# A two-layer graph kernel: adjacency passes of 512 neighbouring columns instead of two far panels of 256, ScalarE copies the first ten Z tiles, weight preparation cut into pieces, the first attention panels' relu issued two chunks ahead

## The reference

```
deg = max(rowsum(adj != 0), 1)
x   = layernorm(x + relu(((adj + I) @ x / deg + x) @ W + b))       # layer 0 (degree factor on both sides)
h   = x @ W_sa;  sl = h @ a_left;  sr = h @ a_right
e   = where(adj != 0, exp(-leaky_relu(sl[:, None] + sr[None, :], 0.01)), 0)
x_a = (e / (rowsum(e) + 1e-5)) @ h
x_b = adj @ (x @ W_gcnb) + b_gcnb
ga  = sigmoid([adj @ x, x] @ Wa + ba);  gb = sigmoid([adj @ x, x] @ Wb + bb)
out = layernorm(x + sigmoid(ga * x_a + gb * x_b))
```

## Time and profile before

| quantity | before |
|---|---|
| median of 3 timed executions | 945.04 us (943.79 to 945.75) |
| profiled execution, its own time | 944.09 us |
| profiled execution, span from first to last instruction | 942.3 us |
| PE busy | 901.3 us (96%) |
| DVE busy | 640.2 us (68%) |
| ACT busy | 459.7 us (49%) |
| POOL busy | 87.4 us (9%) |
| DMA, share while the adjacency is read (slices 5 to 13) | 0.8 to 0.9 |

### The profile page before, as it was taken

One profiled execution on the slowest core, in us unless ns is written; L12 is line 12 of the kernel. 1 busy time (PEld: TensorE's weight loads), 2 busy tenths in 40 slices (PEclk: granted clock), 3 DMA queues, 4 the chain that ended last, 5 costly groups with the idle time before them and its releaser, 6 DMA issues.

```text
span 942.3 us, 20464 instructions
## 1 busy us (share of the span) xinstructions
PE 901.3 (96%) x7829; PEld 783.3 (83%) x7829; DVE 640.2 (68%) x1432; ACT 459.7 (49%) x642; POOL 87.4 (9%) x139
## 2 busy tenths in 40 slices
PE   7995799999999999979999999999999999999996
PEld 6874688888888888858888888888888888888885
DVE  6576555544554446777998797797797797797762
ACT  2653455455455324655656365365355455455450
POOL 1020212222212210000000000000000000000000
PEclk8998999999999999979999999999999999999999
DMA  9978899999999400102201110111111211101000
GB/s 303 273 239 266 285 308 329 311 306 338 300 312 332 165 18 18 52 1 74 73 19 68 61 49 35 61 40 44 61 30 54 61 27 56 61 22 59 15 24 12
DMA packets 95784, 121.65 MB, mean 129 GB/s; under 512 B 6480, under 2 KB 91504, under 8 KB 91632
## 3 DMA queue, kind: packets, MB, share of 16 engines
q1 hardware_dynamic: 91120, 116.69, 37.8%
q10 hardware_dynamic: 4608, 4.20, 1.3%
HBM read 95.69 MB, written 25.18 MB: 128 GB/s over the span
## 4 chain that ended last, share of the span: by engine, by line
PE 82%; DVE 9%; ACT 3%; issue 3%; DMA 2%; POOL 0%; SPq 0%; DVEq 0%; ACTq 0%; POOLq 0%
PE ps L1148 32%; PE ps L1031 22%; PE ps L1110 20%; PE ps L1066 4%; DVE ec L866 3%; PE ps L1014 3%; DVE em L875 1%; ACT ec L516 1%; ACT em L519 1%; DMA strip<-in_adj_dram 1%; DMA xs<-in_x_dram 1%; DVE y L640 1%; PE ps L1051 1%; PE ps L1003 1%; DVE codes L600 0%
## 5 line engine op out<-in xcount | busy, mean ns | idle before, releaser
L1148 PE MATMUL ps<-fb,em 128*128 128x257 f16 x3072 | 346.5, 275 | 8.1 <-DVE em L875 8.1
L1148 PEld LDWEIGHTS ps<-fb,em 128*128 128x128 f16 x3072 | 301.4, 98 | 50.9 <-issue 8.6
L1031 PE MATMUL ps<-y,codes 128*128 128x257 f16 x2048 | 245.9, 276 | 11.7 <-DVE lnst L766 7.8
L1031 PEld LDWEIGHTS ps<-y,codes 128*128 128x128 fp8e4 x2048 | 201.8, 99 | 44.9 <-DVE lnst L766 8.1
L1110 PE MATMUL ps<-fa,pan 128*128 128x258 f16 x2048 | 232.4, 273 | 0.9 <-DVE slrow L834 0.9
L1110 PEld LDWEIGHTS ps<-fa,pan 128*128 128x128 fp8e4 x2048 | 199.2, 97 | 30.7 <-DVE slrow L834 1.2
L866 DVE SCALAR_TENSOR_TENSOR ec<-slb,sr,pan 128x256 f32<-128x256 f32 x512 | 207.9, 478 | 7.6 <-issue 7.3
L516 ACT ACTIVATE ec<-ec,sc 128x2048 f32<-128x2048 f32 x64 | 127.9, 1999 | 131.1 <-DVE ec L866 131.1
L875 DVE SCALAR_TENSOR_TENSOR em<-ec,em 128x2048 f16<-128x2048 f32 x64 | 146.4, 2287 | 16.6 <-ACT em L519 16.5
L519 ACT ACTIVATE em<-ec 128x2048 f16<-128x2048 f32 x64 | 122.3, 1911 | 8.2
L738 DVE TENSOR_SCALAR lnst<-ps 128x1 f32<-128x1 f32 x32 | 5.0, 157 | 107.9 <-PE ps L1031 107.9
(11 more groups left out here) (99 smaller groups left out, 503.0 us busy)
## 6 DMA issues: line engine op xcount, KB each, us to landing
strip<-in_adj_dram SPq DMA_DIRECT2D x128, 512.0 KB, 6.2
a_scratch<-codes SPq DMA_DIRECT2D x16, 1024.0 KB, 8.4
pan<-a_scratch SPq DMA_DIRECT2D x16, 1024.0 KB, 5.0
x_scratch<-x ACTq DMA_DIRECT2D x32, 128.0 KB, 4.7
x1r<-x_scratch SPq DMA_DIRECT2D x32, 128.0 KB, 2.1
out_dram<-ot SPq DMA_DIRECT2D x32, 128.0 KB, 1.7
xs<-in_x_dram SPq DMA_DIRECT2D x3, 1024.0 KB, 11.0
slb<-sl_scratch SPq DMA_DIRECT2D x16, 128.0 KB, 4.7
```

The source lines that it names most:

```text
L1031: mm = pe.matmul(ACC(n), codes[:, qq % SLOTS, h, jb, e * P:(e + 1) * P].bitcast(F8), y[:, jb, part, :], start=(jb == 0 and part == 0), sto ...
L1148: mm = pe.matmul(PH(b)[:, 0:HC], em[slot][:, e_part, jb, (b % 2) * P:(b % 2 + 1) * P], fb[:, jb, h_part, :], start=(jb == 0 and e_part + h ...
```

## The change

Passes now hold 512 neighbouring columns (panels 2qq and 2qq + 1), so a strip is two row blocks of 512 columns where it was four of 256, tiles follow in natural order, and `TILES` is gone. SP sends both halves of a pass's codes to DRAM together, after the pass's last strip. A row block of pass 0 now needs one strip for all four tiles. ScalarE copies Z of tiles 0 to 9 (`ZACT`), VectorE of the rest, after all six `x_max` and `z_scale`. `y_hi` and `y_lo` catch up two a step and then follow two tiles behind. `OUTER` is 16 in place of 24: pass 0 sums row blocks 16 to 31 after the ramp. The weight steps are called at t = 18 to 22, 26, 28, 29 and 30. The first transpose and projection stand inside and behind pass 0. In the first two panels of the second layer the order on VectorE is relu(i), then low(i - 2), across both panels.

The sizes, and the strips and codes on SP:

```
-SJ = 4
+SJ = 2
+ZACT = 10
-OUTER = 24
+OUTER = 16
...
-                sp.dma_start(strip[:, s % RING], adj_view[:, g * SJ:(g + 1) * SJ, c0:c0 + PW]
+                sp.dma_start(strip[:, s % RING], adj_view[:, g * SJ:(g + 1) * SJ, qq * 2 * PW:(qq + 1) * 2 * PW]
...
-                if s >= RING and ends(s - RING):
-                    codes_when_cast(s - RING)
+                if s >= RING and (s - RING) % GS == GS - 1:
+                    codes_when_cast((s - RING) // GS)
```

On ScalarE and VectorE, which `y` parts fall in a step, and ScalarE's steps and what follows them:

```
+        def split_at(t):
+            upto = lambda i: 0 if i < ZACT else min(i - 1, 2 * (i - ZACT) + 2)
+            return range(upto(t - 1), T if t == T else upto(t))
...
             for t in range(T):
                 xt_copy(t)
-                if t >= YLAG:
-                    y_hi(t - YLAG)
-                if 8 <= t < 24 and t % 2 == 0:
+                if 1 <= t <= ZACT:
+                    z_copy(t - 1)
+                for i in split_at(t):
+                    y_hi(i)
+                if 9 <= t < 25 and t % 2 == 1:
                     cast(1)
...
-            cast(6)
-            for n in range(3):
-                normalize(n)
+            cast(4)
+            normalize(0)
             cast(2)
+            x1t_copy(0)
+            normalize(1)
+            cast(2)
+            proj_copies(0)
```

On VectorE, the ramp and what follows it:

```
-            for c in range(4):
+            for c in range(len(XCUT) - 1):
                 x_max(c)
-            for t in range(T):
+            st.sync()
+            dve.tensor_reduce(sc[:, XMX], sc[:, XM], AX, ALU.max).then_inc(S["xmax_part"], 1)
+            z_scale()
+            for t in range(ZACT, T):
                 z_copy(t)
-                if t >= YLAG:
-                    y_lo(t - YLAG)
+                for i in split_at(t):
+                    y_lo(i)
+                if 18 <= t < 22:
+                    weight_column((t - 18) // 2, t % 2)
                 if t == 22:
-                    weight_columns()
+                    weight_squares()
                 if t == 26:
                     weight_norm()
-                if t == 30:
+                if t == 28:
                     weight_scale()
+                if t in (29, 30):
+                    weight_parts(t - 29)
...
-            cast(6)
-            for n in range(3):
-                head(n)
+            cast(2)
+            head(0)
+            cast(2)
+            head(1)
```

On TensorE, the end of the ramp and of pass 0:

```
-                if t - 1 >= ZLAG:
+                if 0 <= t - 1 - ZLAG < OUTER:
                     pass0_rows(t - 1 - ZLAG)
-            for jb in range(T - ZLAG, OUTER):
-                pass0_rows(jb)
             pe.wait_ge(S["ylo_ready"], T)
             for n in range(PT):
                 sum_rows(n, OUTER, T)
+                if n == 2:
+                    t_step(0)
+            p_step(0)
```

More of the change, by code:

```diff
@@ L55 @@
 PER_PAIR = 4 * 5
-TILES = [2 * q + h * (T // 2) + e for q in range(NQ) for h in range(2) for e in range(2)]
 BASE = 16512
@@ L302, in _ @@
                 sp.dma_start(slb[:, m, :], sl0d[m * PW:(m + 1) * PW].partition_broadcast(P)).then_inc(slb_in[m], 16)
-            for s in range(NSTRIP - RING, NSTRIP):
-                if ends(s):
-                    codes_when_cast(s)
+            codes_when_cast(NQ - 1)
             sp.wait_ge(S["slrow_ready"], 1)
@@ L429, in xt_copy, with z_copy @@
                 act.copy(xt[:, t % 2, :], XTP(t)).then_inc(S["xt_ready"], 1)
+            def z_copy(t):
+                act.wait_ge(S["z_done"], t + 1)
+                act.copy(zf[:, t, 0:D], ZP(t)).then_inc(S["zf_act"], 1)
             def y_hi(t):
-                act.wait_ge(S["zf_ready"], t + 1)
+                z_is_copied(act, t)
                 if t == 0:
@@ L568, in _ @@
             for e in range(2):
-                gates(e, 0, 0, e)
+                gates(e, 0, e)
                 gated(e, e)
@@ L684, in weight_scale, with weight_parts @@
                 dve.tensor_scalar(sc[:, INVA], sc[:, IAL], 1.0 / EDGE_VAL, None, ALU.mult).then_inc(S["alpha_ready"], 1)
+            def weight_parts(part):
+                st.sync()
+                if part == 0:
+                    st.then(dve.tensor_scalar(wps[:, :, 0, :], wp[:], sc[:, WS], None, ALU.mult))
+                else:
+                    dve.scalar_tensor_tensor(out=wps[:, :, 1, :], in0=wp[:], scalar=sc[:, WS], in1=wps[:, :, 0, :],
+                                             op0=ALU.mult, op1=ALU.subtract).then_inc(S["wps_ready"], 1)
@@ L771, in head, with parts_lo @@
                 stats(n)
-            cast(6)
-            for n in range(3):
-                head(n)
+            def parts_lo(n):
+                g_lo(n)
+                h_lo(n)
             cast(2)
-            for n in range(PT, T + 3):
-                if n == PT:
-                    x1t_lo(0)
-                    head(3)
-                    g_lo(0)
-                    h_lo(0)
-                    x1t_lo(1)
-                    cast(2)
-                    continue
-                if n == PT + 1:
-                    g_lo(1)
-                    h_lo(1)
-                    x1t_lo(2)
-                    head(4)
-                    g_lo(2)
-                    h_lo(2)
-                    x1t_lo(3)
-                    cast(2)
-                    continue
+            head(0)
+            cast(2)
+            head(1)
+            cast(2)
+            x1t_lo(0)
+            head(2)
+            cast(2)
+            head(3)
+            parts_lo(0)
+            x1t_lo(1)
+            cast(2)
+            parts_lo(1)
+            x1t_lo(2)
+            parts_lo(2)
+            x1t_lo(3)
+            head(4)
+            cast(2)
+            for n in range(PT + 2, T + 3):
                 more = n // PT + 1 < NQ and n < T
@@ L1016, in z_step, with rows_cast @@
                 mm.then_inc(S["z_done"], 1)
-            def rows_cast(qq, h, jb):
-                s = next(i for i in range(NSTRIP) if strip_at(i) == (qq, h, jb // SJ))
-                mine = 0 if on_act(s) else 1
-                pe.wait_ge(S[("cast_act", "cast_dve")[mine]], casts_until(s)[mine])
+            def rows_cast(qq, jb):
+                strip_nr = qq * GS + jb // SJ
+                mine = 0 if on_act(strip_nr) else 1
+                pe.wait_ge(S[("cast_act", "cast_dve")[mine]], casts_until(strip_nr)[mine])
             def sum_rows(n, j0, j1):
@@ L1104, in a_rows @@
             def a_rows(b, slot, j0, j1):
-                for j in range(j0, j1):
-                    jb = TILES[j]
+                for jb in range(j0, j1):
                     for part in range(2):
                         mm = pe.matmul(PA(b)[:, 0:GC], pan[:, slot, jb, (b % 2) * P:(b % 2 + 1) * P].bitcast(F8),
-                                       fa[:, jb, part, :], start=(j == 0 and part == 0),
-                                       stop=(j == T - 1 and part == 1))
+                                       fa[:, jb, part, :], start=(jb == 0 and part == 0),
+                                       stop=(jb == T - 1 and part == 1))
                 return mm
```

208 lines of the change are left out of this document (88 added, 120 removed).

## The result

The changed kernel takes 929.92 us in the median (929.85 to 929.98, 4 runs) beside 945.27 (943.79 to 945.75, 4 runs) for the kernel before: a ratio of 0.984, 95% interval 0.9823 to 0.9857. The forecast was 929.5, with 921 to 938 as its range. The profiled execution has a span of 928.1 us where it was 942.3, and a mean granted clock of 0.988 where it was 0.983.

A forecast was written before the change was run, and what follows sets the result against it. TensorE was busy 901.3 of 942.3 us, so nearly all to win lay in its 41 idle us. 944.09 less 15.9 (up to tile 6) plus 0.4 (second layer) gave 928.6; with 0.95 for the median, 929.5, range 921 to 938.

The forecast's parts named there:

- Ramp to z12: Start of the ramp: with ScalarE copying Z, z12 starts at 24.7 instead of 28.26, 3.6 us won.
- z12 to z31: Later ramp: 16 paces of 1.98 us bring z28 at 56.3; z29 and z30 follow at 57.4 and 58.5.
- The power: GpSimd's power near the ramp's end: ends at 62.2, VectorE waits 4.3 us, all `y_lo` done at 68.6.
- The reading that in the ramp the gap starts at the end of this sum: GpSimd in the ramp: power ends 9.8 us after L359's end at 52.5; counting from the maximum also gave 62.2.
- Rest of pass 0: After the ramp up to tile 6: it starts at 106.1, with 0.2 us waiting at the second projection; 15.9 us won.
- the last lands near 87, in front of the third head's end: Handover after pass 0: the last of strips 22 to 31 arrives near 87, before the third head ends.
- about 4 us from a freed buffer to landing: Handover strips 22 to 31: each takes about 4 us from freed buffer to landing, one coming in 1.5 us.
- The rival of the sticky handover: Handover after pass 0: late strips make TensorE wait twice, some 3.5 us each; win falls about 7, 936.5 us; chance 0.16.
- Passes: Steady passes: tile pitch stays 8.73 us and VectorE's cast 689 ns, nothing on the path either way.
- the slower rival: Steady passes: codes leaving as one 2 MB piece delay strips and stall all six passes, 950.5 us at 3.5 each; chance 0.05.
- Second layer: Its first panels: waits of 2.2, 2.0 and 4.3 us, 2.4 lost to clock; net -0.4, between -1.5 and +2.0.
- Sum: Whole kernel: 944.09 - 15.9 + 0.4 = 928.6 us for the profiled execution, 929.5 for the median of timed runs.

The follow-up runs named there:

- the warmed power: Changed kernel plus one unused GpSimd power after the last maximum over partitions, before the second layer's loop: 925.35 us, ratio 0.978.
- the first experiment: Changed kernel with the weight scale and both weight parts moved behind the last `y_lo`: 928.15 us, ratio 0.9814.
- the fourth version: Changed kernel with late weight steps, casts through the ramp (ScalarE's last behind the last `y_hi`) and an unused GpSimd power before layer two's loop: 917.61 us, ratio 0.9716.
- the last pair: the fourth version, 917.61 us, and the same kernel with `OUTER = 20` in place of 16, 917.05 us.

## Why the prediction was right, point by point

**Ramp to z12.** Forecast 24.7, measured 23.87: the first cast started at 18.24 and the last piece of the maximum at 16.89, both sooner than the rate of 348 GB/s had given. The experiment that undoes the copies confirms the place and the direction.

**z12 to z31.** The pace stayed at 1.98 and z28 stood at 55.63 against 56.3.

**The power.** Right in kind and too large in size. It ended at 60.05, not at 62.2, and VectorE waited 2.56 us, not 4.3, since the gap was 7.78 us and not 9.24 and the sum over partitions ended at 51.67 and not 52.5. The reading that in the ramp the gap starts at the end of this sum is shown; its length was taken from one execution, and it varies from 7.36 to 9.05. The last y was done at 65.84 and not 68.6: 2.15 of the 2.8 us are the power's, 0.45 the first weight part's, which took 0.75 us where 1.2 was taken.

**Rest of pass 0.** Wrong in the handover, and saved by the term before it. The second projection waited 2.09 us where I had 0.2, and 1.7 us more went to half clock. The step that failed is "the last lands near 87, in front of the third head's end". The last strip was there at 85.6, even a little sooner, but the third head had ended at 82.51 and VectorE stood still for 2.22 us, with the fourth head and `x1t_lo` behind the cast. The "about 4 us from a freed buffer to landing" is near the least in the trace of before (3.8, with 6.2 in the median); from 60 to 100 us the changed kernel's strips took 7.0 in the median. With 2.8 us won at y, 0.4 less lost to the clock behind it and 3.6 more lost here, 106.3 becomes 106.7; the trace has tile 6 at about 106.8. The rival of the sticky handover had the mechanism at about half of its price.

**Passes.** 8.73 us a tile, as forecast; 702 ns a cast against the 689 kept. TensorE has no stall between 107 and 350 us, so codes in one piece of 2 MB cost nothing: the slower rival is out.

**Second layer.** The net of the stretch was -0.6 where -0.4 stood: 2.12, 2.06 and 4.46 us of waiting, 2.7 at half clock, against 2.2, 2.0, 4.3 and 2.4. Neither sign is clear of the 3 us by which this stretch differs between executions. And the cause of the last wait was wrong, as the warmed power shows.

**Sum.** 15.16 us up to the second layer against 15.9, and 929.92 against 929.5. The near hit is in part luck. For the profiled execution the sum gave 928.6, and it took 929.98; the 0.95 us added for the median was not there, which leaves 0.4 of the 1.4. And behind it stand two errors of about 3 us with opposite signs, at two places that pass work to each other: the experiment with the late scale shows that what is won at the first is in large part waited for at the second.

## What to carry to other kernels

Ask of each in-order engine what stands behind an instruction that waits for a transfer or for a slow first use; here moving one cast behind two short high parts was worth 3.5 to 4 us, and one unused instruction 5 to 7. Look in the trace for where the engine is set up for the new kind of instruction, ahead of a wait or behind it. Where two stalls follow one another and the second is set by transfers, a gain at the first is given back, and only edits to both show their worth. One trace tells which wait there is, not what it is worth: compare versions by their timed executions and the intervals of these.

## What was not expected of the hardware

GpSimd was silent for 6.8 to 9.05 us (9.24 before) ahead of its first power after a sum or maximum over partitions, counted from the MODIFY_POOL_CONFIG of the power's line, which in the ramp stands right behind the sum and in the second layer's loop 56 us behind the maximum, after the wait for the input; in the ramp an unused power whose input is long ready didn't shorten it. Why it was 7.36 in one execution and 9.05 in another is open. The same program took 927.43 to 933.17 us in five executions. Within the profiled ones the stretches at half clock lie at differing places, behind waits of 2 to 6 us, and some waits of that size have none behind them (2.23 us in the first experiment, 2.77 in the fourth version). That they make the spread is likely but not shown, since there is one profile for each kernel. In the last pair the profiled executions were the fastest and the slowest of their fives: their traces differ by 4.1 us (344.38 and 348.49 at the second layer's start) where the medians differ by 0.6.
